# Attention scores of two heads at a time, in two PSUM banks, with new issue orders

## The chip, the cores and the metric

The kernel runs on one core of a Trainium2 chip. The time is the device time of one execution in microseconds (us), the median of three runs. TensorE is called PE here, VectorE DVE, ScalarE ACT, GpSimd POOL, and SyncE, which issues the DMAs, SP.

## What is computed

The input is x, 16 sequences of 512 rows and 128 columns, in float32. A state space block (a Mamba layer) comes first, with a normalisation before and after it, and two attention layers with feed-forward follow.

```python
x = x + _layernorm(_L0_attn_ref(_layernorm(x), ...))   # projections, convolution, a scan over 512 steps, 256 channels x 16 states
x = x + _layernorm(_L0_ffn_ref(_layernorm(x), ...))    # two layers of the kind below
# in a layer: 8 heads of 64; every block of 64 queries looks at its own 64 keys and the 64 before
sim = einsum('bhwid,bhwjd->bhwij', bq, bk)
sim = where(mask, -big, sim)
attn = softmax(sim)
out = einsum('bhwij,bhwjd->bhwid', attn, bv)
x = x + o @ wo
h = a * gelu(g)        # a, g: the halves of layernorm(shift_token(x)) @ w1 + b1
x = x + h @ w2 + b2
```

## The kernel before

The work on one sequence is cut into four streams. **E** (enter) normalises, projects and convolves, and writes the inputs of the scan to DRAM. **M** (state) is the scan: 32 steps, each an exponential on ACT (line 591), a product on POOL (643), the scan itself on DVE (615) and a second product on POOL (660), with a sum on PE (568) after every four; it ends with a normalisation into `xs`. **A** (front, the object `wf`, tiles named `f_bank`) is attention and feed-forward of layer 0, and **B** (back, `wb`, tiles named `b_bank`) the same of layer 1, and the store of the result.

In round k the kernel runs B on sequence k, A on k + 1, M on k + 2 and E on k + 3, for k from -3 to 15, so there are 14 rounds (k = 0 to 13) with A, B and M, of which the last has no E; round 14 has A and B alone, and round 15 only B. Each engine is a queue that runs strictly in the order in which the kernel issues, and `ORDER` gives that order for every engine: `A4 B1` stands for four steps of A, then one of B. `weave` carries it out. A step waits on semaphores for what it needs, and all that stands behind it on its engine waits too.

The rounds are tied to each other in four ways. A's first step, the turn of x at line 345, needs the last addition of A's feed-forward of the round before (1010) and M's normalised rows (340). B keeps its queries, keys and one bank in tiles that E uses as well: E's first PE step, the turn into `b_bank`, needs B's addition of the attention's result (line 899, `x_added`), and B of the next round needs the rows that E stored (`spilled`, the DMAs at 374 and 377). M of the next round reads these rows back before its first product.

A layer's attention has three PSUM banks (`w.banks`). For projections and rotations they are used in turn. Then they are S, PT and O. For each of eight heads PE writes the mask into S (703, bf16) and adds the scores (708): four tiles of 128 queries, each as two products with 64 rows of weights and 64 columns, that is a half of the array's rows, since a head is 64 wide, and the two halves of its columns in turn. DVE takes the row maxima (879), ACT the exponentials (818), PE turns them into PT (345), DVE or ACT copies them out (887 for even heads, 826 for odd ones), PE multiplies with the values into O (730), and DVE divides (892, 895). The scores of head i + 1 wait for the exponentials of head i, because both use S. Even heads use the first 64 partitions of keys and queries, and odd heads the last 64.

After the heads come four turns of the result (345) and their copies (830), the product with `wo` (743) and the addition (899).

Of the kernel before, what the change touches and what calls it, by code (L numbers as in the profile page):

```python
# [10 lines left out]
ALU = mybir.AluOpType  # L11
ACT = mybir.ActivationFunctionType
# [3 lines left out]
P = 128  # L16
# [30 lines left out]
    "act": (  # L47
# [4 lines left out]
    "dve": (  # L52
# [4 lines left out]
    "pool": (  # L57
        "A3 M2 A1 M1 B1 M2 A1 M2 B3 M1 B1 M2 A1 M1 B1 A1 B1 M2 B1 M1 A1 B1 A1 M2 B2 A1 B1 A1 B2 A1 B2 A1 M1 A1 M1 "
        "A1 M1 A1 M47 B1 M1 E4"),
    "sp": "M18 E1 M3 B2 S3 M1 S2",  # L60
# [40 lines left out]
def build(nc, a, out):  # L101
    with ExitStack() as ctx:
# [50 lines left out]
        class Attention:  # L153


            def __init__(self, n, banks, pr):
# [26 lines left out]
                self.scored, self.peaked, self.weighed = s("scored", 8), s("peaked", 8), s("weighed", 8)  # L183
# [492 lines left out]
        def pe_attention(E, e, b, w, l, x):  # L676
# [17 lines left out]
            S, PT, O = w.banks  # L694
            ot = O[:, 0:NT * (DH + 1)].rearrange("p (t d) -> p t d", t=NT)
            for i in range(HEADS + 2):
                if i < HEADS:
                    c, r = i // 2, DH * (i % 2)
                    if i == 0:
                        E.wait_ge(*w.qk_copied(b, 7))  # L700
                    else:
                        E.wait_ge(*w.weighed(b, i - 1))
# [542 lines left out]
```

## Time and profile before

| | |
|---|---|
| Median of three runs | 2666.77 us (2666.22 to 2666.95) |
| The profiled execution | 2667.45 us |
| Its span in the trace | 2665.7 us |
| PE, DVE, ACT, POOL busy | 2060.1, 1988.5, 1832.8, 1788.4 us |
| A full round in the middle | about 150 us |

The shares of busy time are averages over rounds with several stages. Busy time of PE is modelled at the ends of its matmuls, and a few of its records are missing. The sum below is made against 2667.45 us; the median lies 0.7 us under it.

### The profile page before, as it was taken

What the parts mean: (1) busy time and instruction counts of PE and PEld (TensorE: products, weight loads), DVE (VectorE), ACT (ScalarE), POOL (GpSimd) and SP (SyncE); (2) the same over time, 40 slices, a digit from 0 to 9 for tenths busy, and PEclk for the clock granted to TensorE, in tenths of its full rate; (3) what the DMA queues carried; (4) which work ended last, traced back from release to release, by engine and by line L of the source; (5) the groups of instructions that cost most, each with busy time, mean ns of one, the idle gap of its engine ahead of it and who ended that gap; (6) DMA issues with size and microseconds to landing.
All of it is one profiled execution on the core that took longest, in us unless ns stands there. A gap on an engine that the chain in (4) does not pass through costs nothing. (4 is left out here: it accounts for less than half of the span.)

```text
span 2665.7 us, 44136 instructions
## 1 busy us (share of the span) xinstructions
PE 2060.1 (77%) x15779; PEld 1248.1 (47%) x15936; DVE 1988.5 (75%) x3765; ACT 1832.8 (69%) x3953; POOL 1788.4 (67%) x1668
## 2 busy tenths in 40 slices
PE   2146788797978888796979888797979888786966
PEld 0013355463636455463636455463636455463734
DVE  1457696978879696978878796978878796977442
ACT  2244778787777778687777878687867878676443
POOL 0859595867859595867868595867859595863010
PEclk8567999898989999999999999999999999999877
DMA  3534323324333323324333323324333323320000
GB/s 113 142 99 107 102 74 97 97 70 120 92 112 94 96 70 100 95 69 120 92 112 92 100 68 96 94 73 119 93 112 88 100 72 93 95 72 9 5 5 8
DMA packets 107147, 231.27 MB, mean 87 GB/s; under 512 B 7728, under 2 KB 48688, under 8 KB 106672
## 3 DMA queue, kind: packets, MB, share of 16 engines
q1 hardware_dynamic: 106928, 228.44, 31.2%
q8 instruction: 126, 2.06, 0.3%
q14 instruction: 93, 0.76, 0.1%
HBM read 185.42 MB, written 42.99 MB: 86 GB/s over the span
## 5 line engine op out<-in xcount | busy, mean ns | idle before, releaser
L660 POOL TENSOR_TENSOR gy<-hs,bc 128x512 f32<-128x512 f32 x512 | 650.2, 1270 | 196.4 <-DVE hs L615 135.5
L615 DVE TENSOR_TENSOR_SCAN hs<-da,dbu 128x512 f32<-128x512 f32 x512 | 622.3, 1215 | 83.2 <-POOL dbu L643 51.4
L643 POOL TENSOR_TENSOR dbu<-spread,bc 128x512 f32<-128x512 f32 x512 | 650.3, 1272 | 22.4 <-DMA spread<-steps 22.1
L591 ACT ACTIVATE da<-spread,rest 128x512 f32<-128x512 f32 x512 | 353.3, 690 | 237.4 <-DVE hs L615 222.5
L914 POOL TENSOR_TENSOR kr<-kr,rn 128x512 f32<-128x512 f32 x256 | 264.3, 1041 | 46.4 <-ACT rn L786 35.4
L686 PE MATMUL f_bank<-rest,h_t 128*128 128x512 f32 x384 | 232.5, 707 | 70.4 <-DVE kr L859 49.2
L838 DVE TENSOR_REDUCE ss<-sq 128x8 f32<-128x512 f32 x256 | 172.4, 673 | 97.0 <-ACT sq L765 95.2
L686 PE MATMUL b_bank<-rest,h_t 128*128 128x512 f32 x384 | 227.9, 701 | 18.0 <-ACT h_t L755 12.3
L568 PE MATMUL y_sum<-gy,rest 128*32 128x512 f32 x1024 | 144.2, 637 | 96.4 <-POOL gy L660 96.4
L818 ACT ACTIVATE late<-b_bank,mx 128x128 f32<-128x128 f32 x512 | 145.9, 368 | 71.0 <-DVE mx L879 68.8
L345 PE MATMUL f_bank<-first,kr 128*128 128x128 f32 x768 | 119.8, 288 | 96.4 <-DVE kr L859 91.6
L345 PE MATMUL b_bank<-first,kr 128*128 128x128 f32 x768 | 121.4, 294 | 83.1 <-DVE kr L859 73.4
L1068 POOL TENSOR_TENSOR sq<-xs,sq 128x512 f32<-128x512 f32 x16 | 20.2, 1265 | 244.5 <-ACT xs L340 244.5
L708 PE MATMUL b_bank<-k_t,q_t 64*64 64x128 f32 x2048 | 148.6, 287 | 39.7 <-issue 15.8
L818 ACT ACTIVATE sq<-f_bank,mx 128x128 f32<-128x128 f32 x512 | 145.2, 369 | 35.3 <-DVE mx L879 35.2
L88 ACT ACT_TABLE_LOAD x112 | 143.7, 1283 | 32.9 <-DVE mv_enter L318 12.2
L345 PEld LDWEIGHTS b_bank<-first,kr 128*128 128x128 f32 x768 | 87.9, 148 | 163.4 <-DVE kr L859 124.4
L345 PEld LDWEIGHTS f_bank<-first,kr 128*128 128x128 f32 x768 | 89.3, 145 | 151.1 <-DVE kr L859 126.7
L708 PE MATMUL f_bank<-k_t,q_t 64*64 64x128 f32 x2048 | 145.8, 284 | 13.9 <-issue 5.4
L686 PEld LDWEIGHTS f_bank<-rest,h_t 128*128 128x128 f32 x384 | 75.2, 221 | 158.3 <-DVE kr L859 69.9
L686 PEld LDWEIGHTS b_bank<-rest,h_t 128*128 128x128 f32 x384 | 79.5, 225 | 119.5 <-issue 59.4
L879 DVE TENSOR_REDUCE mx<-b_bank 128x4 f32<-128x512 f32 x128 | 87.9, 687 | 59.1 <-PE b_bank L708 59.1
(176 smaller groups left out, 5009.2 us busy)
## 6 DMA issues: line engine op xcount, KB each, us to landing
spread<-steps SPq DMA_DIRECT2D x256, 512.0 KB, 4.6
steps<-k_t SPq DMA_DIRECT2D x32, 512.0 KB, 3.1
bc<-bc_rows SPq DMA_DIRECT2D x32, 512.0 KB, 7.8
gate<-gates SPq DMA_DIRECT2D x32, 512.0 KB, 5.3
gates<-kr SPq DMA_DIRECT2D x16, 512.0 KB, 3.4
gates<-late SPq DMA_DIRECT2D x16, 512.0 KB, 4.3
sq<-in_x SPq DMA_DIRECT2D x16, 256.0 KB, 3.3
x<-in_x SPq DMA_DIRECT2D x16, 256.0 KB, 4.9
```

The source lines that it names most:

```text
L88: self.e.preload_act_table_set(name)
L345: op = e.transpose(bank[:, n * P:(n + 1) * P], src(n), ident[:, :])
L568: op = e.matmul(y_sum[32 * j:32 * j + 32, :], sel[:, w, :], gy[:, 2 * j + k, :], start=w == 0 and k == 0, stop=w == 1 and k == 1, skip_gro ...
L591: e.activation(da[:, :], spread[:, slot(b, s // 2), 0, :], ACT.Exp, scale=a_neg[:, s:s + 1]).then_inc(decayed.sem, 1)
L615: e.tensor_tensor_scan(hs[:, s % 2, :], da[:, :], dbu[:, s % 2, :], 0.0, ALU.mult, ALU.add).then_inc(scanned.sem, 1)
L643: e.tensor_tensor(dbu[:, s % 2, :], spread[:, slot(b, s // 2), 1, :], bc[:, s % 2, :], ALU.mult).then_inc(fed.sem, 1)
L660: e.tensor_tensor(gy[:, s % 8, :], hs[:, s % 2, :], bc[:, 2 + s % 2, :], ALU.mult).then_inc(read_out.sem, 1)
L686: e.matmul(bank[:, :], w.h_t[:, t * P:(t + 1) * P], wqkv[:, l, part * INNER:(part + 1) * INNER], start=True, stop=True).then_inc(w.project ...
L708: op = e.matmul(S[WIN * j:WIN * j + WIN, p * P:(p + 1) * P].rearrange("p (a n) -> p a n", a=2), w.q_t[r:r + DH, c, q0:q0 + WIN], keys if j ...
L818: op = e.activation(w.pr[:, i % 2, p, :], S[:, p * P:(p + 1) * P], ACT.Exp, bias=w.mx[:, i, p:p + 1])
L838: e.tensor_reduce(w.ss[:, n, :], heads(w.sq[:, n % 2, :]), AX, ALU.add).then_inc(w.summed.sem, 1)
L914: e.tensor_tensor(x, x, w.rn[:, n, :].unsqueeze(2).to_broadcast([P, HEADS, DH]), ALU.mult).then_inc(w.normed.sem, 1)
```

## The change

The scores of heads 2g and 2g + 1 are now one step, `score(g)`. The two heads have a bank each, `X[0]` and `X[1]`, the former S and PT. PE writes the mask into both, and then issues for each tile of queries four products: two halves of columns for the even head, whose keys and queries lie in the first 64 partitions, and two for the odd head in the last 64. They use the four quarters of the array. A head's exponentials are turned into the bank in which its scores were (`turn`), and are copied out from there. `score(g)` therefore waits until the copies of both heads of the pair before are done (`p_ready`), where the scores of a head waited for the exponentials of the one before. The semaphore `scored` counts pairs. `value(hd)` holds the eight products with the values as before, `peak(hd)` and `share(hd)` the maxima and the division. Every `ORDER` string is new. The numbers of instructions on DVE, ACT and POOL for this work are the same, and PE's too.

```diff
 ORDER = {
...
-    "sp": "M18 E1 M3 B2 S3 M1 S2",
+    "sp": "M17 E1 M3 S2 M1 B1 S3 M1 B1",
...
@@ pe_attention @@
-            S, PT, O = w.banks
+            X, O = w.banks[0:2], w.banks[2]
...
+            def score(g):
+
+                if g == 0:
+                    E.wait_ge(*w.qk_copied(b, 7))
+                else:
+                    E.wait_ge(*w.p_ready(b, 2 * g - 2))
+                    E.wait_ge(*w.p_ready(b, 2 * g - 1))
+                for i in range(2):
+                    e.matmul(X[i][:, :], identb[:, :], maskb[:, :], start=True, stop=False, skip_group_check=True)
+                for p in range(NT):
+                    for j in range(2):
+                        for i in range(2):
+                            q0, r = p * P + WIN * j, DH * i
+                            keys = w.k_t[r:r + DH, g, q0:q0 + P].rearrange("p (a n) -> p a n", a=2)
+                            op = e.matmul(X[i][WIN * j:WIN * j + WIN, p * P:(p + 1) * P].rearrange("p (a n) -> p a n", a=2),
+                                          w.q_t[r:r + DH, g, q0:q0 + WIN], keys if j else keys[:, ::-1, :], start=False,
                                           stop=True, skip_group_check=True)
+                op.then_inc(w.scored.sem, 1)
+
+            def turn(hd):
+                E.wait_ge(*w.weighed(b, hd))
+                pe_turn(e, X[hd % 2], lambda n: w.pr[:, hd % 2, n, :]).then_inc(w.p_turned.sem, 1)
...
+            score(0)
+            yield
+            for g in range(HEADS // 2):
+                turn(2 * g)
+                yield
+                turn(2 * g + 1)
+                yield
+                value(2 * g)
+                yield
+                if g + 1 < HEADS // 2:
+                    score(g + 1)
                     yield
...
+                value(2 * g + 1)
+                yield
@@ act_attention @@
...
+                    op = e.activation(w.pr[:, hd % 2, p, :], X[hd % 2][:, p * P:(p + 1) * P], ACT.Exp,
+                                      bias=w.mx[:, hd, p:p + 1])
...
+                    e.activation(w.p_t[:, 1, :], X[1][:, :], ACT.Copy).then_inc(w.p_copied_act.sem, 1)
@@ dve_attention @@
...
+            for hd in range(0, HEADS, 2):
+                peak(hd)
+                yield
+                peak(hd + 1)
+                yield
+                if hd:
+                    yield from share(hd - 1)
...
+                e.tensor_copy(w.p_t[:, 0, :], X[0][:, :]).then_inc(w.p_copied.sem, 1)
+                yield
+                yield from share(hd)
+            yield from share(HEADS - 1)
```

Three places show how the new orders move instructions. The first is PE early in the heads of stream B. `b_bank<-maskb` and `b_bank<-k_t,q_t` are mask and scores, `b_bank<-first,late` is the turn of a head's exponentials, `b_bank<-vs,m` and `<-v,m` the product with the values, `f_bank` is the same for stream A. Before, from B's second head on:

```order
L703 MATMUL b_bank<-maskb,identb 128x512
L708 MATMUL b_bank<-k_t,q_t 64x128 x8
L345 MATMUL f_bank<-first,kr 128x128 x4
L345 MATMUL b_bank<-first,late 128x128 x4
L345 MATMUL f_bank<-first,kr 128x128 x4
L703 MATMUL b_bank<-maskb,identb 128x512
L708 MATMUL b_bank<-k_t,q_t 64x128 x8
L703 MATMUL f_bank<-maskb,identb 128x512
L708 MATMUL f_bank<-k_t,q_t 64x128 x8
L345 MATMUL b_bank<-first,late 128x128 x4
```

And of after, from B's second pair on:

```order
L706 MATMUL b_bank<-maskb,identb 128x512 x2
L712 MATMUL b_bank<-k_t,q_t 64x128 x16
...
L345 MATMUL f_bank<-first,kr 128x128 x4
L345 MATMUL b_bank<-first,late 128x128 x4
L345 MATMUL f_bank<-first,kr 128x128 x4
L345 MATMUL b_bank<-first,late 128x128 x4
L345 MATMUL f_bank<-first,kr 128x128 x4
```

Stream A's scores now begin after B's third pair, where they began behind B's third head.

The second place is PE at the end of stream A's heads. `b_bank<-first,q_t` is the turn with which stream E begins, `L433` its first projection, `f_bank<-first,sq` the turn of the exponentials of A's last head, `f_bank<-first,kr` the turns of A's result and `L743`, later `L757`, the product with `wo`. Before:

```order
L568 MATMUL y_sum<-gy,rest 32x512 x4
L345 MATMUL f_bank<-first,sq 128x128 x4
L345 MATMUL b_bank<-first,q_t 128x128 x4
L730 MATMUL f_bank<-vs,m 64x65
L730 MATMUL f_bank<-v,m 64x65
...
L433 MATMUL b_bank<-m,first 128x512
L730 MATMUL f_bank<-vs,m 64x65
```

And of after, where the first row belongs to the value product of A's last head:

```order
L730 MATMUL f_bank<-vs,m 64x65
...
L345 MATMUL f_bank<-first,kr 128x128 x8
L345 MATMUL b_bank<-first,q_t 128x128 x4
L345 MATMUL f_bank<-first,kr 128x128 x8
L433 MATMUL b_bank<-m,first 128x512
L757 MATMUL f_bank<-rest,q_t 128x128 x16
L345 MATMUL b_bank<-first,sq 128x128 x4
L958 MATMUL f_bank<-xs,rest 128x256
```

The turn of E moved from between A's last turn and its last two value products to behind the whole of A's last head and two turns of the result.

The third place is ACT at the end of a round. `L483`, `L488` and `L491` belong to E's step sizes, the rows on `kr` (990, later 1011) are A's gelu, `mv_y` and `mv_x` M's statistics, `mv_out` those of B's result. Before:

```order
L88 ACT_TABLE_LOAD
L990 ACTIVATE kr<-f_bank,rest 114x512 x2
L483 ACTIVATE m<-b_bank,first 128x512
L990 ACTIVATE kr<-f_bank,rest 113x512
L88 ACT_TABLE_LOAD
L488 ACTIVATE m<-m 128x512 x2
L491 ACTIVATE m<-m 128x512 x2
L325 ACTIVATE lv_x<-mv_x,columns 128x4
L329 ACTIVATE rs_x<-lv_x 128x4
L340 ACTIVATE xs<-x,mr_x,rs_x 128x128 x4
```

And of after:

```order
L491 ACTIVATE m<-m 128x512 x2
L88 ACT_TABLE_LOAD
L1011 ACTIVATE kr<-f_bank,rest 114x512
L1011 ACTIVATE kr<-f_bank,rest 113x512
L88 ACT_TABLE_LOAD
L325 ACTIVATE lv_x<-mv_x,columns 128x4
L325 ACTIVATE lv_out<-mv_out,columns 128x4
L329 ACTIVATE rs_out<-lv_out 128x4
L329 ACTIVATE rs_x<-lv_x 128x4
L340 ACTIVATE xs<-xs,mr_out,rs_out 128x128 x4
L340 ACTIVATE xs<-x,mr_x,rs_x 128x128 x4
```

E's exponentials and logarithms moved ahead of A's last two gelus, B's last normalisation moved to directly before M's, and a full round has six table loads in place of seven.

## Rows read from the trace of the kernel before

**Rows 1.** The page, part 1: busy us (share of the span), instructions.

```profile
PE 2060.1 (77%) x15779; PEld 1248.1 (47%) x15936; DVE 1988.5 (75%) x3765; ACT 1832.8 (69%) x3953; POOL 1788.4 (67%) x1668
```

**Rows 2.** Timeline, start of two rounds: start, us, engine, line, [idle<-releaser].

```profile
1060.19 0.63 PE L345 MATMUL f_bank<-first,xs 128*128 128x128 f32 x4 [0.87 <-DVE xs L1010]
1065.64 0.63 PE L345 MATMUL b_bank<-first,xs 128*128 128x128 f32 x4 [0.70 <-DMA steps<-k_t]
...
1208.72 1.65 ACT L340 ACTIVATE xs<-x,mr_x,rs_x 128x128 f32<-128x128 f32 x4 [0.29 <-DVE mr_x L334]
1209.70 0.69 DVE L1010 TENSOR_TENSOR xs<-xs,f_bank 128x512 f32<-128x512 f32 x1 [1.08 <-PE f_bank L961]
1210.54 0.63 PE L345 MATMUL f_bank<-first,xs 128*128 128x128 f32 x4 [0.87 <-DVE xs L1010]
1212.25 0.36 SPq L377 DMA_DIRECT2D steps<-k_t  x1
```

**Rows 3.** Busy by stretch: us, PE, PEld, DVE, ACT, POOL (x instructions), PEclk, DMA.

```profile
1060.20:1114.90 54.70, 37.97 (x140) 17.95 (x145) 48.81 (x72) 35.65 (x73) 44.01 (x50) 0.91 0.42 113
1114.90:1172.00 57.10, 51.22 (x673) 37.93 (x683) 49.60 (x96) 44.59 (x116) 51.69 (x43) 1.00 0.40 105
1172.00:1210.50 38.50, 35.19 (x178) 20.14 (x178) 24.45 (x66) 34.10 (x60) 16.11 (x14) 1.00 0.15 50
```

**Rows 4.** Timeline: first maxima, E's turn, A's last value product and wo.

```profile
1114.93 0.69 DVE L879 TENSOR_REDUCE mx<-b_bank 128x4 f32<-128x512 f32 x1 [0.22 <-PE b_bank L708]
...
1167.35 0.66 PE L345 MATMUL b_bank<-first,q_t 128*128 128x128 f32 x4
...
1171.77 0.22 PE L730 MATMUL f_bank<-v,m 128*64 128x65 f32 x1
```

**Rows 5.** Timeline: one head of stream B.

```profile
1116.85 0.39 PE L703 MATMUL b_bank<-maskb,identb 128*128 128x512 bf16 x1 [0.97 <-ACT late L818]
1117.17 1.09 PE L708 MATMUL b_bank<-k_t,q_t 64*64 64x128 f32 x16
1118.31 0.69 DVE L879 TENSOR_REDUCE mx<-b_bank 128x4 f32<-128x512 f32 x1 [0.23 <-PE b_bank L708]
1119.04 1.14 ACT L818 ACTIVATE late<-b_bank,mx 128x128 f32<-128x128 f32 x4 [0.16 <-DVE mx L879]
```

**Rows 6.** Groups by line and shape: busy us, mean ns, idle before.

```profile
L708 PE MATMUL b_bank<-k_t,q_t 64*64 64x128 f32 x2048 | 148.6, 287 | 39.7 <-issue 15.8 <-ACT late L818 12.1 <-ACT k_t L794 9.8
L615 DVE TENSOR_TENSOR_SCAN hs<-da,dbu 128x512 f32<-128x512 f32 x512 | 622.3, 1215 | 83.2 <-POOL dbu L643 51.4 <-issue 15.9 <-ACT da L591 14.5
L313 DVE BATCH_NORM_STATS2 stat_ff<-sq 128x6 f32<-128x128 f32 x128 | 27.8, 279 | 40.9 <-ACT sq L973 40.9
L88 ACT ACT_TABLE_LOAD x112 | 143.7, 1283 | 32.9 <-DVE mv_enter L318 12.2 <-DVE mv_out L318 6.2 <-PE b_bank L952 3.3
```

**Rows 7.** Waits of DVE from 1114.9 to 1172: us in total, times, longest.

```profile
DVE mx L879 <- PE b_bank L708: 1.9, 5, 0.7
DVE mx L879 <- PE f_bank L708: 1.2, 3, 0.7
```

**Rows 8.** Round 14, timeline of DVE: first maxima of B, last division of A.

```profile
2458.95 0.69 DVE L879 TENSOR_REDUCE mx<-b_bank 128x4 f32<-128x512 f32 x1 [2.01 <-PE b_bank L708]
...
2517.65 0.18 DVE L892 RECIPROCAL rd<-f_bank 128x4 f32<-128x4 f32 x1 [0.87 <-PE f_bank L730]
```

**Rows 9.** Busy by stretch in rounds 14 and 15, as rows 3.

```profile
2460.00:2480.00 20.00, 18.19 (x144) 14.04 (x148) 6.99 (x13) 7.98 (x27) 1.04 (x1) 0.57 0.01 1
...
2590.60:2628.00 37.40, 32.26 (x278) 24.63 (x279) 12.53 (x26) 11.18 (x36) 0.00 (x0) 0.52 0.00 1
```

**Rows 10.** Round 15, timeline of DVE: the maxima, then the last division.

```profile
2590.68 0.69 DVE L879 TENSOR_REDUCE mx<-b_bank 128x4 f32<-128x512 f32 x1 [5.60 <-PE b_bank L708]
2595.16 0.69 DVE L879 TENSOR_REDUCE mx<-b_bank 128x4 f32<-128x512 f32 x1 [3.79 <-PE b_bank L708]
...
2628.13 0.18 DVE L892 RECIPROCAL rd<-b_bank 128x4 f32<-128x4 f32 x1 [0.87 <-PE b_bank L730]
```

More of the change, by code:

```diff
@@ new lines, in turn, with value @@
+            def turn(hd):
+                E.wait_ge(*w.weighed(b, hd))
+                pe_turn(e, X[hd % 2], lambda n: w.pr[:, hd % 2, n, :]).then_inc(w.p_turned.sem, 1)
+            def value(hd):
+                E.wait_ge(*w.p_ready(b, hd))
+                E.wait_ge(*w.v_paired(b, NT - 1))
+                E.wait_ge(*w.v_before(b, NT - 2))
+                if hd:
+                    E.wait_ge(*w.o_done(b, hd - 1))
+                for p in range(NT):
+                    for j in range(2):
+                        q0 = p * P + WIN * j
+                        op = e.matmul(ot[WIN * j:WIN * j + WIN, p, :], w.p_t[:, hd % 2, q0:q0 + WIN],
+                                      (w.vs, w.v)[j][:, p, hd, :], start=True, stop=True)
+                op.then_inc(w.valued.sem, 1)
@@ L808, in act_attention @@
                     yield
-            S, PT, O = w.banks
-            for i in range(HEADS + 1):
-                if i < HEADS:
-                    E.wait_ge(*w.peaked(b, i))
-                    if i > 1:
-                        E.wait_ge(*w.p_turned(b, i - 2))
-                    E.use_table(EXP_LN)
-                    for p in range(NT):
-                        op = e.activation(w.pr[:, i % 2, p, :], S[:, p * P:(p + 1) * P], ACT.Exp, bias=w.mx[:, i, p:p + 1])
-                    op.then_inc(w.weighed.sem, 1)
-                    yield
-                hd = i - 1
-                if hd > 0 and hd % 2:
+            X = w.banks[0:2]
+            for hd in range(HEADS):
+                E.wait_ge(*w.peaked(b, hd))
+                if hd > 1:
+                    E.wait_ge(*w.p_turned(b, hd - 2))
+                E.use_table(EXP_LN)
+                for p in range(NT):
+                    op = e.activation(w.pr[:, hd % 2, p, :], X[hd % 2][:, p * P:(p + 1) * P], ACT.Exp,
+                                      bias=w.mx[:, hd, p:p + 1])
+                op.then_inc(w.weighed.sem, 1)
+                yield
+                if hd % 2:
                     E.wait_ge(*w.p_turned(b, hd))
@@ L829, in act_attention @@
                 E.wait_ge(*w.o_turned(b, c))
-                e.activation(w.o_t[:, c, :], (S, PT)[c % 2][:, :], ACT.Copy).then_inc(w.o_copied.sem, 1)
+                e.activation(w.o_t[:, c, :], X[c % 2][:, :], ACT.Copy).then_inc(w.o_copied.sem, 1)
                 yield
@@ new lines, in peak, with share @@
+            def peak(hd):
+                E.wait_ge(*w.scored(b, hd // 2))
+                e.tensor_reduce(w.mx[:, hd, :], X[hd % 2][:, :].rearrange("p (t k) -> p t k", t=NT), AX, ALU.max,
+                                negate=True).then_inc(w.peaked.sem, 1)
+            def share(hd):
+                E.wait_ge(*w.valued(b, hd))
+                e.reciprocal(w.rd[:, hd, :], ot[:, :, DH]).then_inc(w.inverted.sem, 1)
+                yield
+                E.wait_ge(*w.inverted(b, hd))
+                e.tensor_tensor(w.o[:, :, hd * DH:(hd + 1) * DH], ot[:, :, 0:DH],
+                                w.rd[:, hd, :].unsqueeze(2).to_broadcast([P, NT, DH]), ALU.mult).then_inc(w.o_done.sem, 1)
+                yield
@@ new lines, in dve_attention @@
+            for hd in range(0, HEADS, 2):
+                peak(hd)
+                yield
+                peak(hd + 1)
+                yield
+                if hd:
+                    yield from share(hd - 1)
+                E.wait_ge(*w.p_turned(b, hd))
+                if hd:
+                    E.wait_ge(*w.valued(b, hd - 2))
+                e.tensor_copy(w.p_t[:, 0, :], X[0][:, :]).then_inc(w.p_copied.sem, 1)
+                yield
+                yield from share(hd)
+            yield from share(HEADS - 1)
```

69 lines of the change are left out of this document (5 added, 64 removed), and 22 rows, old and new, of the table ORDER.

## The prediction, written before the run

> **What bounds the kernel now.** The busy shares come first: PE 77%, DVE 75%, ACT 69%, POOL 67% [rows 1]. No engine is full, so the question is what ties the rounds together. The timeline where two rounds meet answers it. A full round is 1210.54 - 1060.19 = 150.3 us. At its end three chains arrive almost at once: M's normalised rows (1208.72 + 1.65 = 1210.37), the end of A (1209.70 + 0.69 = 1210.39), and E's last store, issued at 1212.25, for whose like B's first turn waited at 1065.64 [rows 2]. Shortening one chain alone gives nothing.
>
> I cut the round at two places, B's first row maxima (1114.93) and A's last product with the values (ends at 1172.0) [rows 4], and read the busy time of each stretch [rows 3]. Stretch 1 (54.7 us) is projections and rotations: DVE is busy 48.8 us, PE only 38.0. Stretch 2 (57.1 us) holds all heads: PE 51.2, POOL 51.7, DVE 49.6. Stretch 3 (38.5 us) is the feed-forward of both layers, nearly all of E and the end of M: PE 35.2, ACT 34.1, DVE 24.5. The change shortens PE's work in stretch 2, where it is one of three nearly full engines, and moves work among all three.
>
> **PE's work.** One head's scores are 16 records of mean 287 ns that together take 1.09 us [rows 5, 6]: the two column halves already run side by side. In no row do two halves of the array's rows run side by side. If the second head of a pair is hidden whole, a pair costs 1.09; if not at all, 2.18. I take 1.09, since the column halves hide each other whole, and keep 2.18 as a rival. The Trainium skill's page TensorEngine Tiling (Array Packing), section Theoretical Speedup, gives up to a factor of two for each dimension of 64 or less; by the columns alone, which is all that the trace shows, nothing would be saved, and by the page the second factor comes too. With 1.09, eight pairs a round save 8 x 1.09 = 8.7 us of PE. The masks cost the same as before, 0.32 each [rows 5].
>
> **The waits of a pair.** Before, two heads in a row take 2 x (0.32 + 1.09 + 0.69 + 1.14) = 6.5 us of mask, scores, maxima and exponentials [rows 5], 6.7 with the hops. Now it is two masks, one set of scores, the first maxima, two heads' exponentials, the odd head's turn (0.66, rows 4) and its copy, which I price like the maxima, a pass over the same 512 columns: 0.64 + 1.09 + 0.69 + 2.28 + 0.66 + 0.69 = 6.1, 6.3 with hops. The new wait on `p_ready` thus costs no time against the old one, 0.4 us less a pair. Behind the waiting scores on PE stand the values of the odd head and A's steps; DVE waits for them.
>
> **Stretch 1.** Two of A's rotation steps on DVE, 0.66 each, come after B's first maxima instead of ahead of them. DVE's 48.8 becomes 47.5. Around it lie the start-up (A's first projection and square, some 3.7 us in which DVE has nothing) and some 1.5 us for B's last keys. That gives 52.7, so -2.0. Bounds: 0 and -2.5.
>
> **Stretch 2.** DVE gains the two rotation steps (+1.3) and loses one scan (-1.2, rows 6) and B's feed-forward statistics (four of 0.28 and the small steps behind them, -1.6, rows 6), so 49.6 - 1.5 = 48.1 us. Its idle time was 57.1 - 49.6 = 7.5 us, of which 3.1 waited for scores [rows 7]. With PE at 51.2 - 8.7 = 42.5 us, PE no longer presses and most of that 3.1 goes; the rest stays, because A's last two pairs now run without B beside them and each is a chain of 6.3 us and more. I take 4.8 us idle: 52.9, so -4.2. Bounds: 3 us idle (-6.0) and 7.5 (-1.5).
>
> **Stretch 3.** Before, E's turn started at 1167.35, 4.6 us ahead of the cut [rows 4], and from there to the next round's start it is 43.2 us [rows 2, 4]. Now the turn stands behind A's last values and two turns of its result. DVE must first do a scan (1.2) and the last division, then PE two turns: 2.7 us behind the cut. The chain from there loses one table load of 1.28 (seven a round, 112 in 16 [rows 6], become six). The result is 2.7 + 43.2 - 1.3 = 44.6, so +6.1. For: E's exponentials stand ahead of A's last gelus. Against: B's last normalisation stands directly ahead of M's on ACT, and A's now follows SiLU of E. I keep 42 and 47 as bounds. The new place of B's result on POOL, last in the round, costs nothing: POOL is busy 16.1 of 38.5 us there [rows 3].
>
> A round: -2.0 - 4.2 + 6.1 = -0.1 us. PE's 8.7 us are gained in stretch 2 only as far as DVE allows and are given back by E's late start. Fourteen rounds: -1 us.
>
> **The last two rounds** have no M and no E, so DVE's limit and E's late start are both absent. In round 15 B runs alone at half clock (0.52, that is mostly 1.2 of 2.4 GHz [rows 9]). Maxima follow each other in 4.5 us (2590.68, 2595.16), and to the last division it is 37.4 us [rows 10]. A pair was 9.0 and is now 1.2 (masks) + 1.97 (scores at half clock, an estimate from 1.09) + 0.69 + 2.28 + 1.1 + 0.69 = 7.9, 8.1 with hops. Three pairs and the end of the fourth (some 6) give 30.3: -7. In round 14 the same stretch is 58.7 us [rows 8], 20 us of it at clock 0.57 with PE busy 18.2 [rows 9]. Now A's scores start after two of B's pairs and the third's scores (some 16 us), three pairs of A follow at some 8.5, and the fourth takes some 7: 49, so -10. Bounds -4 and -15. Together -17.
>
> **Forecast**: 2667.45 - 1 - 17 = 2649; against the median 0.7 less, 2648 us.
>
> **The rivals.**
>
> *The cut comes through.* DVE's idle time in stretch 2 falls to 3 us and stretch 3 is 43: a round is -2 - 6 + 4.5 = -3.5, and the time 2667 - 49 - 17 = 2601. For it speaks that PE is busy 35.2 of 38.5 us in stretch 3, so that whatever it sheds ahead helps. Against it, DVE.
>
> *E starts late and nothing is made up* (the slower side). E's chain goes through every engine in order. If the table load saved does not lie on it, and A's normalisation and last gelus wait behind E's SiLU and B's gelu, stretch 3 is 47: a round is +2.3, the sum +32 - 17 = +15, 2682 us. It is slower than before from 45.9 us of stretch 3 on. The three arrivals within 2 us [rows 2] speak for it.
>
> *The row halves do not overlap.* A pair costs 1.09 more, DVE keeps 7.5 us idle, a round is +2.6, and in the last round a pair is 10.1 against 9.0. That gives 2667 + 36 + 4 = 2707.
>
> *The clock falls in the heads.* It fell to 0.57 and 0.52 where M and E were absent [rows 9], and stretch 2 now has less of PE's work. If half of a round's heads run at 1.2 GHz as in round 14, some 8 us of PE come back: +3.5 a round, 2667 + 49 - 10 = 2706. Against it, stretch 1 with PE busy 38.0 of 54.7 keeps 0.91 [rows 3].
>
> **How the numbers follow.** Chances: forecast (2627 to 2662) 0.40, cut comes through 0.19, E late 0.23, no overlap 0.08, clock 0.10. The range reaches from 2603 to 2697: it leaves out nearly half of the first rival and most of the last two, 0.2 in all. About 0.2%, 5 us, is what can be told from no change. Faster by more than that: 0.38 of the forecast's 0.40 and the first rival's 0.19, so 0.57. Within it: the forecast's rest and the near end of E late, 0.11. Slower: 0.32. Cases of both signs share the chance; the likeliest one's own range is 2627 to 2662.
>
> **What would show it.** Right: 32 score records of a pair within some 1.1 us; PE's busy time 120 to 150 us less; stretches near 52.7, 52.9 and 44.6; E's turn behind A's last values; 96 table loads; round 15 shorter by 7 us. Wrong: a score step of 2 us; clock under 0.95 in stretch 2; a stretch 3 under 42 us or over 47.

## The result, and the profile after

The kernel after takes 2584.3 us (2582.7 to 2585.6, 4 runs) against 2666.5 (2664.9 to 2667.0, 4 runs) for the kernel before beside it: a ratio of 0.969, 95% interval 0.968 to 0.971. The forecast was 2648 with a range from 2603 to 2697. The gain is 82 us where 19 were forecast, and the time lies 19 us below the range.

Page of the kernel after, part 1 (busy us, share of the span, instructions) and the granted clock in 40 slices; they answer to [rows 1]:

```profile
PE 1929.1 (75%) x15808; PEld 1115.1 (43%) x15936; DVE 1973.0 (76%) x3765; ACT 1786.7 (69%) x3937; POOL 1785.1 (69%) x1668
PEclk9986899999999999998999999999999999999977
```

PE is busy 131 us less (120 to 150 were forecast). Beyond that DVE is down 15.5 us and ACT 46, of which 20.5 are sixteen table loads.

The round that answers to [rows 3], cut at the same places (round start, B's first maxima, end of A's last value product, next start). Columns: us, PE, PEld, DVE, ACT, POOL with instructions, granted clock, DMA share, GB/s:

```profile
1039.40:1091.00 51.60, 33.50 (x141) 15.01 (x143) 47.01 (x72) 32.68 (x67) 41.19 (x46) 0.97 0.43 107
1091.00:1141.70 50.70, 44.68 (x665) 31.46 (x671) 46.46 (x87) 39.42 (x107) 48.12 (x43) 1.00 0.38 100
1141.70:1184.80 43.10, 37.15 (x185) 21.27 (x186) 28.32 (x78) 39.06 (x73) 22.31 (x18) 1.00 0.25 81
```

A round is 145.4 us: 51.6 + 50.7 + 43.1. Against 54.7 + 57.1 + 38.5 that is -3.1, -6.4 and +4.6. The forecast had -2.0, -4.2 and +6.1. All three signs are right, and all three sizes err to the same side. Over the thirteen full rounds (0 to 12) the means are 54.4, 56.8 and 38.7 before and 51.7, 50.8 and 43.0 after: -2.7, -6.0 and +4.3. The round shown in [rows 3] has a longer second stretch than most (57.1 where 56.7 is usual).

The pair of heads, the timeline of PE and DVE (start, us, engine, line), against [rows 5]:

```profile
1096.77 0.38 PE L706 MATMUL b_bank<-maskb,identb 128*128 128x512 bf16 x1 [0.16 <-issue]
1097.08 1.10 PE L712 MATMUL b_bank<-k_t,q_t 64*64 64x128 f32 x32
...
1098.25 1.29 DVE L892 TENSOR_REDUCE mx<-b_bank 128x4 f32<-128x512 f32 x2
```

The 32 records of a pair take 1.10 us, as the 16 of one head took 1.09: the halves of the rows hide each other whole.

Where two rounds meet, the timeline of PE, SyncE's queue and POOL, against [rows 2, 4]:

```profile
1143.86 0.60 PE L345 MATMUL b_bank<-first,q_t 128*128 128x128 f32 x4
...
1180.71 0.36 SPq L377 DMA_DIRECT2D steps<-k_t  x1
...
1184.75 0.63 PE L345 MATMUL f_bank<-first,xs 128*128 128x128 f32 x4 [0.87 <-DVE xs L1031]
1185.21 0.60 PE L345 MATMUL b_bank<-first,xs 128*128 128x128 f32 x4
...
1193.57 1.27 POOL L643 TENSOR_TENSOR dbu<-spread,bc 128x512 f32<-128x512 f32 x1 [9.56 <-DMA spread<-steps]
```

E's turn does stand 2.2 us behind the cut, but E's last store is issued 36.9 us after it (1180.71 - 1143.86), where it took 44.9 before (1212.25 - 1167.35 [rows 2, 4]). So it comes 4.0 us ahead of the next round's start; before, it came 1.7 behind it. B's first turn follows A's at once (1185.21), where it waited for that store's data until 5.4 us after the start [rows 2]. A's start itself waits for A's own sum for 0.87 us in both kernels, so the store sets when B starts, and not when A does.

The two last rounds, where heads run without M and E (stretches from B's first maxima to the last division; round 14, then 15), against [rows 8 to 10]:

```profile
2390.13 1.29 DVE L892 TENSOR_REDUCE mx<-b_bank 128x4 f32<-128x512 f32 x2 [0.57 <-PE b_bank L712]
...
2436.28 0.18 DVE L898 RECIPROCAL rd<-f_bank 128x4 f32<-128x4 f32 x1 [0.93 <-PE f_bank L730]
```

And of the stretches:

```profile
2390.00:2436.00 46.00, 39.47 (x627) 30.55 (x632) 26.31 (x59) 28.21 (x87) 2.95 (x4) 1.00 0.01 2
2513.70:2542.30 28.60, 19.65 (x259) 14.41 (x262) 11.89 (x26) 11.09 (x36) 0.00 (x0) 0.74 0.00 1
```

They are 46.2 and 28.6 us where 58.7 and 37.4 were: -12.5 and -8.8, forecast -10 and -7. Between the two stretches 4.4 us are given back: from A's last division in round 14 to B's maxima in round 15 (2513.72) it is 77.4 us for 73.0, at a granted clock of 0.79 for 0.87.

The whole difference follows from the round starts. These are A's first turns in rounds 0 and 13 of the kernel before, then of after:

```profile
312.36 0.66 PE L345 MATMUL f_bank<-first,xs 128*128 128x128 f32 x4 [1.21 <-ACT xs L340]
2261.59 0.63 PE L345 MATMUL f_bank<-first,xs 128*128 128x128 f32 x4 [0.87 <-DVE xs L1010]
```

```profile
313.00 0.63 PE L345 MATMUL f_bank<-first,xs 128*128 128x128 f32 x4 [0.87 <-DVE xs L1031]
2204.56 0.63 PE L345 MATMUL f_bank<-first,xs 128*128 128x128 f32 x4 [0.87 <-DVE xs L1031]
```

Thirteen full rounds took 1949.2 us and take 1891.6: -57.6, -4.4 each. The spans end at 2665.7 and 2580.2, so what follows them took 404.1 us and takes 375.6: -28.5. What precedes them is the same within 1 us. (The spans differ by 85.5 us, the medians by 82.)

What follows is rounds 13 to 15, and round 13 is a case of its own: it has A, B and M, but no E. It took 148.6 us and takes 139.3, so -9.3, and the last two rounds together -19.1. The forecast counted round 13 among fourteen rounds of -0.1 us. So it missed 56 us in the full rounds, 9 in round 13 and 2 in the last two. The third stretch of round 13, before and then after, in the columns of [rows 3]:

```profile
2373.10:2410.20 37.10, 30.35 (x164) 19.86 (x164) 18.95 (x58) 25.34 (x44) 13.20 (x11) 0.94 0.07 22
```

```profile
2306.60:2343.80 37.20, 29.22 (x166) 18.13 (x165) 21.90 (x69) 26.64 (x52) 16.83 (x14) 1.00 0.12 30
```

Without E this stretch does not grow, though DVE has 3 us more to do in it and ACT 1.3. With E it grows by 4.3 us. (The granted clock is 0.94 in one and 1.00 in the other, so a part of a microsecond may be hidden in this.)

### The profile page after: what moved, and what is told of

Read it like the earlier page. It is cut to its first block, busy times and chain, and to the rows that moved or that the text cites. A ratio compares the mean times of both kernels' runs of the same rounds, so it can differ in the third digit from the quotient of the medians.

```text
span 2580.2 us, 44117 instructions
## 1 busy us (share of the span) xinstructions
PE 1929.1 (75%) x15808; PEld 1115.1 (43%) x15936; DVE 1973.0 (76%) x3765; ACT 1786.7 (69%) x3937; POOL 1785.1 (69%) x1668
## 4 chain that ended last, share of the span: by engine, by line
POOL 25%; DVE 25%; ACT 18%; PE 16%; issue 9%; DMA 5%; SPq 1%; POOLq 0%; DVEq 0%; ACTq 0%
POOL gy L660 9%; POOL dbu L643 8%; DVE hs L615 7%; POOL kr L935 5%; ACT late L831 3%; ACT da L591 3%; DMA x<-in_x 3%; DVE mx L892 3%; PE b_bank L345 2%; DVE ss L851 2%; PE b_bank L712 2%; DVE m L860 2%; PE f_bank L345 2%; ACT sq L831 2%; ACT L88 1%
## 5 line engine op out<-in xcount | busy, mean ns | idle before, releaser
L686 PE MATMUL b_bank<-rest,h_t 128*128 128x512 f32 x384 | 238.9, 733 | 93.9 <-DVE kr L872 76.1
L686 PE MATMUL f_bank<-rest,h_t 128*128 128x512 f32 x384 | 213.9, 662 | 25.9 <-ACT h_t L769 14.0
L671 POOL TENSOR_TENSOR x<-gy,x 128x512 f32<-128x512 f32 x16 | 20.4, 1276 | 191.0 <-DVE gy L628 191.0
L345 PE MATMUL f_bank<-first,sq 128*128 128x128 f32 x576 | 93.4, 285 | 24.0 <-ACT sq L831 23.9
L345 PE MATMUL b_bank<-first,late 128*128 128x128 f32 x512 | 81.1, 287 | 34.9 <-ACT late L831 34.9
```

What stands on the lines that cost most here:

```text
L345: op = e.transpose(bank[:, n * P:(n + 1) * P], src(n), ident[:, :])
L686: e.matmul(bank[:, :], w.h_t[:, t * P:(t + 1) * P], wqkv[:, l, part * INNER:(part + 1) * INNER], start=True, stop=True).then_inc(w.project ...
```

## The experiments

The kernel before took 2657 to 2663 us in the four groups of runs, and a second run of the kernel after agrees with the first.

> The kernel after itself, unchanged, on the chip of this job, as the base for the three others. If chips differ little, 2584 us as at first, a ratio of 0.969 to 0.971; if the kernel after is touchier than the one before (the kernel before takes 2657 to 2667 on three chips), up to 2600.

Measured 2582.0 us, ratio 0.971 (0.968 to 0.973). I compare with 2583 us below. Most rounds of the kernel after repeat to 0.2 us (51.6, 50.7, 43.1), so that stretches tell more than times. In some variants rounds of two lengths take turns; where that matters it is said.

**1. The heads in turn, not side by side.**

```diff
-                for p in range(NT):
-                    for j in range(2):
-                        for i in range(2):
+                for i in range(2):
+                    for p in range(NT):
+                        for j in range(2):
```

> The changed kernel, with all orders and banks as they are, but the eight score products of the even head stand on PE ahead of the eight of the odd head, so that the two heads' row halves no longer take turns. If PE's time in the heads is what the change is worth (theory Q, the quarters), a score step takes about 2.0 us in place of 1.10, PE's busy time grows by some 8 x 16 x 1.0 = 130 us, a round grows by 3 to 5 us and the time lies at 2635 to 2665. If the new orders carry the gain (theory O), the time stays within 2584 to 2610. If the halves overlap in this order too, the score step stays near 1.1 us and the time at 2584.

Measured 2639.4 us, ratio 0.992 (0.990 to 0.995). The timeline of PE and the stretches of a round of this kernel:

```profile
968.89 1.59 PE L712 MATMUL b_bank<-k_t,q_t 64*64 64x128 f32 x32
```

And of the stretches:

```profile
910.70:962.70 52.00, 33.83 (x140) 15.36 (x141) 46.99 (x71) 32.79 (x67) 41.52 (x46) 0.97 0.43 106
962.70:1016.30 53.60, 47.81 (x667) 34.99 (x672) 46.87 (x87) 39.38 (x107) 47.74 (x42) 1.00 0.36 95
1016.30:1059.40 43.10, 37.14 (x186) 21.24 (x185) 28.36 (x78) 39.10 (x73) 22.34 (x18) 1.00 0.25 81
```

The same sixteen products take 1.59 us when a head's sixteen records come in a row, 1.10 when the heads alternate. That is 0.49 us x 128 pairs = 63 us of PE, and the time rose by 56: PE's score step has a price of 0.9 us a microsecond. For the 3.9 us of PE added in a round, stretch 2 grows by 2.9 us and stretch 1 by 0.4.

**2. The scores twice.** The sixteen products of a pair are issued once more ahead of the masks.

```diff
+                for p in range(NT):
+                    for j in range(2):
+                        for i in range(2):
+                            ...
+                            e.matmul(X[i][...], w.q_t[...], keys ..., start=True, stop=True, skip_group_check=True)
                 for i in range(2):
                     e.matmul(X[i][:, :], identb[:, :], maskb[:, :], start=True, stop=False, skip_group_check=True)
```

> The kernel after, in which the sixteen score products of a pair are issued a second time ahead of the masks (their result is overwritten by the mask, so the output is the same). A pair costs PE 1.10 us more, 128 pairs in all: 141 us of PE. It is as if the halves of the rows did not overlap. Theory 1: the end of the program follows PE's score step nearly one to one in the heads; with the heads in turn a pair took 1.59 us in place of 1.10 and the time rose 55 us for 63 us of PE, 0.88 a microsecond. Then this kernel takes 2584 + 0.88 x 141 = 2708 us (2690 to 2725). Theory 2: DVE is what limits the heads and PE only touches it: the first half microsecond cost what it did by chance of the order, and the rest is partly hidden: under 2660.

Measured 2710.9 us, ratio 1.020 (1.018 to 1.022). Theory 1 holds: +128 us for 141 of PE, 0.91. Stretch 2 of this kernel:

```profile
1757.10:1814.60 57.50, 52.72 (x896) 37.52 (x896) 47.01 (x87) 39.51 (x107) 47.19 (x42) 1.00 0.34 89
```

+6.8 for 8.8 us of scores, DVE's busy time up by 0.5. PE costs this kernel what the row halves would cost if they did not overlap. So without that overlap the change would be 2% slower than the kernel before, and the rival's 2707 us was near the right price for it.

**3. More work for DVE.**

```diff
                 E.wait_ge(*w.inverted(b, hd))
+                e.tensor_reduce(w.spare[:, hd % 2, :], ot[:, :, 0:DH], AX, ALU.max)
                 e.tensor_tensor(w.o[:, :, hd * DH:(hd + 1) * DH], ot[:, :, 0:DH],
```

> The kernel after, with one more reduction on DVE for each head, ahead of the division, over the 256 elements of the head's values, into a spare tile of its own: 16 a round at about 0.41 us (the division reads as many elements and takes 0.41), 6.6 us of DVE a round, 105 us in all. Theory 1 (the prediction's: DVE is the limit of the second stretch, it idles only 4.2 of 50.7 us there): nearly all of it comes through, 2665 to 2690. Theory 2: the way through the heads is the chain mask, scores, maxima, exponentials, and DVE's work besides it fits in: under 2620.

Measured 2638.0 us, ratio 0.993 (0.991 to 0.995), between the two theories. The added reduction takes 0.42 us, 107 us in all, and 55 of them come through. A round is 149.4 us, its stretch 2:

```profile
964.20:1019.40 55.20, 47.18 (x672) 32.28 (x672) 51.58 (x102) 39.75 (x108) 48.58 (x43) 0.97 0.35 94
```

Here stretch 2 grew by 4.5 us for the 6.7 added (DVE's busy time rose by 5.1, the rest overlaps). But the granted clock is 0.97 in it, and PE is busy 47.2 us for 44.7 with the same work. In some rounds the clock stays at 1.00, and there it is 54.0 us:

```profile
1563.60:1617.60 54.00, 45.97 (x672) 31.44 (x671) 51.48 (x102) 39.80 (x108) 48.49 (x43) 1.00 0.36 97
```

That is +3.3 us for 6.7, the same 0.5 a microsecond as over the whole program, and some 1.2 us of the 4.5 come with the lower clock. DVE has a price too, then, but it is no lid over PE: its idle time is 3.6 us in the first of these rounds and 2.5 in the second, under the 4.8 that the forecast left it.

**4 and 5. Orders and heads apart.** The first kernel has the heads of after and the `ORDER` strings of before (on PE the first pair's scores stand at the place of its first head's and most later ones at that of the second head's, where the expectation has the first for all; each turn stands where it can). The second has the heads of before and the strings of after.

> The changed code of the heads, both banks and the quarters, with the orders of the kernel before: the strings of DVE, ACT, POOL and SP word for word, PE's with the score steps of a pair merged at the place of the first one. Theory Q: PE is relieved as in the changed kernel, and the time is near it, 2584 to 2620. Theory O: it is near the kernel before or above it, 2650 to 2700, because the old orders put A's and B's heads where the new banks make them wait for the copies of a pair.

> The heads of the kernel before, one at a time in one bank, with the orders of the changed kernel: DVE, ACT, POOL and SP word for word, PE's with each pair's score step split into two around the turn. Theory Q: no gain or a loss, 2660 to 2720. Theory O: most of the gain is there, 2590 to 2630.

Measured 2958.1 us, ratio 1.113 (1.110 to 1.116), and 3135.9 us, ratio 1.182 (1.176 to 1.188). Both miss both theories. The stretches of the first:

```profile
1000.60:1054.50 53.90, 37.19 (x157) 17.10 (x162) 48.76 (x73) 36.06 (x74) 44.23 (x50) 0.94 0.43 116
1054.50:1133.70 79.20, 54.76 (x658) 38.36 (x657) 50.65 (x96) 43.23 (x115) 51.81 (x44) 0.81 0.29 75
1133.70:1172.60 38.90, 35.40 (x181) 20.26 (x180) 24.61 (x66) 34.43 (x60) 15.81 (x13) 1.00 0.15 50
```

And of the second:

```profile
871.80:923.10 51.30, 34.40 (x123) 15.70 (x125) 46.97 (x71) 32.62 (x67) 40.87 (x45) 0.93 0.43 108
923.10:1012.30 89.20, 69.67 (x680) 51.54 (x689) 48.06 (x87) 40.24 (x107) 48.52 (x43) 0.75 0.22 57
1012.30:1055.40 43.10, 37.15 (x185) 21.28 (x186) 28.32 (x78) 39.04 (x73) 22.29 (x18) 1.00 0.25 81
```

They cannot price the orders of the heads, since queues in an order made for other steps wait for each other there (and the granted clock falls to 0.81 and 0.75 while PE waits). But they part the terms: stretches 1 and 3 are those of the kernel whose strings they have (53.9 and 38.9 with the old, 51.3 and 43.1 with the new), whatever the heads do. So -3.1 and +4.6 belong to the orders, and only stretch 2 to both.

**6. E's turn early.** On PE the step with E's turn is moved from behind two turns of A's result to ahead of A's last but one value product, about where it was before.

> The changed kernel with one step moved: E's first turn on PE stands ahead of the last two value products of A, where it was before the change. My sum priced its new place at about +6 us a round in the last stretch (stretch 3 was 38.5 us before, is 43.1 now). If the late turn costs that, this kernel gains 2 us or more a round, 2530 to 2560. If the turn is late because ACT and DVE have E's other steps late as well, nothing changes: 2578 to 2590.

Measured 2648.5 us, ratio 0.996 (0.994 to 0.997): 65 us slower than after. The turn in this kernel:

```profile
1025.15 1.12 PE L332 MATMUL b_bank<-first,q_t 128*128 128x128 f32 x4 [3.73 <-ACT q_t L327]
```

And its second stretch:

```profile
973.10:1029.50 56.40, 46.82 (x669) 33.08 (x676) 48.09 (x87) 40.64 (x110) 49.43 (x44) 0.97 0.38 99
```

PE stands 3.7 us in front of the turn, since ACT normalises E's input later in the new order. Behind it stand A's value products. The round starts at 920.69, so the turn comes 104.5 us behind the start, just as in the kernel after (1143.86 - 1039.41): it stands earlier in the queue and comes no earlier. Stretch 2 becomes 56.4 us, stretch 3 41.7, so 5.7 are lost ahead of the cut for 1.4 behind it. About 2 of the 5.7 us come with the clock, since PE is busy 46.8 us for 44.7 at a granted clock of 0.97. So moving PE's step alone gains nothing; what an earlier start of E as a whole would be worth, this kernel does not show.

**7. The old tail.** Behind A's last head PE, ACT and DVE follow in the order of the kernel before.

> The kernel after, but behind A's last head the steps of PE, ACT and DVE follow in the order of the kernel before (on PE E's turn stands directly behind A's last value product, ahead of the turns of A's result; on ACT seven table loads a round in place of six), and POOL adds B's result ahead of M's. Theory 1: in the kernel after E's last store is issued 4 us ahead of the next round's start, so E's chain binds nothing and its earlier turn gives nothing; the new order of the tail is worth the table load and one or two us more for A's feed-forward and M's normalisation: 2584 + 16 x (1.3 to 3) = 2605 to 2632. Theory 2 (the prediction's): E's late turn costs, and the earlier turn gives about 1 us a round less the table load: 2575 to 2595.

Measured 2725.7 us, ratio 1.026 (1.024 to 1.028), worse than either theory. A round of this kernel and the store in question:

```profile
317.60:373.80 56.20, 37.81 (x141) 16.73 (x142) 46.95 (x70) 32.65 (x67) 43.04 (x47) 0.88 0.43 117
373.80:427.10 53.30, 45.75 (x672) 31.52 (x672) 46.77 (x87) 41.04 (x111) 49.24 (x43) 1.00 0.39 105
427.10:472.60 45.50, 38.68 (x186) 22.18 (x185) 27.46 (x78) 38.64 (x70) 19.59 (x16) 0.93 0.12 37
```

And of its timeline:

```profile
474.32 0.36 SPq L364 DMA_DIRECT2D steps<-k_t  x1
```

E's turn comes at 427.50, 1.8 us sooner after the cut, and still the last store is issued 46.8 us behind it (36.9 in the kernel after), 1.7 us behind the next start at 472.60. B's channels come to ACT 8.0 us behind the start (480.62). Stretch 3 is 2.4 us longer, with one more table load of 1.28 in it and a granted clock of 0.93, stretch 2 is 2.6 us longer and stretch 1 4.6. In all this kernel takes 9.6 us more a round. In the kernel with all the old strings (experiment 4) the same tail has a third stretch of 38.9 us, so this, too, is a queue in an order made for other steps, and no price of E's place.

**8. The loads of M ahead of the last store.** In the kernel after M's first product waits for loads that stand behind the store of B's result on the DMA queue.

```diff
-    "sp": "M17 E1 M3 S2 M1 B1 S3 M1 B1",
+    "sp": "M2 O1 M15 E1 M3 S2 M1 B1 S3 M1",
```

(`O` is the store of B's result of the round before.)

> The kernel after, with the store of B's result behind the first loads of M's next round on the DMA queue, where those loads stood behind it (they were issued at 1039.20 and 1039.83, the store at 1038.72, and M's first product on POOL waited 7.6 us for them). The loads need E's last store, which lands about 2.8 us after 1035.39. Theory 1: they are issued up to 1.6 us earlier and the start of the scans follows by as much, or partly: 2560 to 2580. Theory 2: the first stretch is set by A's and B's projections and rotations on DVE, and the DMA engines are full there anyway (9 tenths and more in most slices): no change, 2580 to 2588.

Measured 2608.9 us, ratio 0.982 (0.980 to 0.984): slower by 26, which neither theory had. Both halves of the reason are in the timeline; the round starts at 1046.41:

```profile
1045.82 0.58 SPq L1100 DMA_DIRECT2D out_dram<-sq  x1
...
1051.50 1.27 POOL L643 TENSOR_TENSOR dbu<-spread,bc 128x512 f32<-128x512 f32 x1 [5.84 <-DMA spread<-steps]
...
1052.10 0.59 ACT L767 ACTIVATE h_t<-b_bank 64x512 f32<-64x512 f32 x1 [1.20 <-DMA out_dram<-sq]
```

M's product is 5.1 us behind the start, 1.8 sooner than in the kernel after at 1039.41 (1046.30), as planned. But the store now lands behind two loads of 512 KB, and ACT, which wants its buffer for B, waits for it until 5.7 us. The same two places in the kernel after, start at 1039.41:

```profile
1038.72 0.38 SPq L1098 DMA_DIRECT2D out_dram<-sq  x1
...
1042.98 0.58 ACT L767 ACTIVATE h_t<-b_bank 64x512 f32<-64x512 f32 x1
```

**9 to 11. The last microseconds, and one load ahead.** First, on DVE A's last two gate steps ahead of the statistics of B's result, and on ACT M's rows ahead of B's:

```diff
-    "dve": "... E1 M1 A1 B1 M1 B2 A2 B1 M1 A1"
+    "dve": "... E1 M1 A1 B1 M1 A2 B2 M1 B1 A1"
-    "act": "... E2 A2 M1 B2 M1 B1 M1"
+    "act": "... E2 A2 M2 B2 M1 B1"
```

(Only the ends of the two strings are shown.)

> The kernel after with another order in the last 6 us of a round: on DVE A's last two gate steps (0.7 each) ahead of the statistics of B's result, on ACT M's normalised rows ahead of B's. Theory 1: the next round starts when A's feed-forward and M's rows are both there (in the kernel after at 1039.27 and 1038.89), and E's chain, whose last store is issued at 1035.39, has no part in it. A's end comes 1.2 us earlier, M's too: 1.2 us a round, 2584 - 17 = 2567 (2562 to 2574). Theory 2: B's result, now 2.2 us later, binds the next round, since the same buffer is wanted by B's first squares and the first loads of M stand behind its store on the DMA queue: 2584 to 2610.

Measured 2604.8 us, ratio 0.979 (0.977 to 0.982). The time fits theory 2: stretch 3 gains less than 1 us, but B's result is late, and with it its store and the loads behind that store. The round starts at 900.83:

```profile
903.16 0.38 SPq L1085 DMA_DIRECT2D out_dram<-sq  x1
...
905.69 0.59 ACT L754 ACTIVATE h_t<-b_bank 64x512 f32<-64x512 f32 x1 [0.42 <-DMA out_dram<-sq]
...
910.97 1.27 POOL L630 TENSOR_TENSOR dbu<-spread,bc 128x512 f32<-128x512 f32 x1 [7.83 <-DMA spread<-steps]
```

M's first product is 10.1 us behind the start, B's channels 4.9 (3.6 in the kernel after), and stretch 1 is 53.6. Second, only the load that depends on nothing late ahead of the store (`"sp": "M1 O1 M16 ..."`); third, both:

> As the kernel with the loads first, but only one load (B's rows of E, which wait for nothing of the last stores) stands ahead of the store of B's result; the loads of the spread steps stand behind it as in the kernel after. With both loads ahead, M's first product came 1.8 us earlier, but the store took over 5 us behind a megabyte of loads, and ACT waited for it until 5.7 us after the round's start. Theory 1 (the store's landing is what cost 24 us): it lands in time here, and the earlier load is worth 0 to 1 us a round: 2568 to 2584. Theory 2 (any load ahead delays the store by about as much as it moves): 2590 to 2610.

Measured 2582.0 us, ratio 0.971 (0.968 to 0.974), the same as after. The harm of experiment 8 was the store's landing. M's first product came 5.1 to 6.7 us behind the starts here, 6.7 to 8.8 in the kernel after, and that gained nothing: so early, M's start is covered.

> The two edits together. If B's late result binds the next round by way of the loads behind its store, the load ahead of it takes part of that back: faster than the new end alone by up to 1 us a round. If both gains come through: 2584 - 17 - 8 = 2559 us. If the store lands too late for B's first squares: slower than the new end alone, 2580 to 2600.

Measured 2592.6 us, ratio 0.975 (0.972 to 0.978): 12 us of the new end's 22 come back. B starts as late as with the new end alone, and M's first product comes at 7.8 us in place of 10.0, so at this point M's start does count. No variant beats the kernel after.

**12. E's last store late.** By itself:

```diff
-    "sp": "M17 E1 M3 S2 M1 B1 S3 M1 B1",
+    "sp": "M17 E1 M3 S2 M1 B1 S2 M1 B1 S1",
```

> The kernel after, in which only E's last store (du) stands behind M's and B's stores on the DMA queue: it is issued at about 0.3 us ahead of the next round's start in place of 4.0 ahead, some 3.7 us later, and lands where that of the kernel before did. Nothing else is moved. Theory 1: the first stretch was 54.7 us in the kernel before and is 51.6 after mainly because the store comes earlier, so that B's first turn need not wait for it and M's first product stands 6.9 us behind the round's start in place of 10.8. Then stretch 1 grows by 2 to 3.5 us and the time by 30 to 52 us: 2613 to 2635. Theory 2 (the prediction's): the stretch is shorter because two of A's rotation steps on DVE come behind B's first maxima; the store's time is hidden: under 2595.

Measured 2623.4 us, ratio 0.985 (0.983 to 0.987), +40 us, in the range of theory 1. A round of this kernel:

```profile
606.30:661.40 55.10, 37.15 (x140) 16.64 (x142) 47.00 (x71) 32.44 (x67) 41.18 (x45) 0.88 0.43 110
661.40:712.10 50.70, 44.70 (x665) 31.50 (x672) 46.45 (x87) 39.37 (x107) 48.12 (x43) 1.00 0.38 100
712.10:755.20 43.10, 37.13 (x186) 21.25 (x185) 28.36 (x78) 39.09 (x73) 22.35 (x18) 1.00 0.22 69
```

And of its timeline:

```profile
610.10 1.08 PE L332 MATMUL b_bank<-first,xs 128*128 128x128 f32 x4 [3.13 <-DMA steps<-k_t]
610.98 2.95 PE L673 MATMUL f_bank<-rest,h_t 128*128 128x512 f32 x4
...
613.56 0.69 DVE L838 TENSOR_REDUCE ss<-sq 128x8 f32<-128x512 f32 x1 [7.20 <-ACT sq L766]
```

Only stretch 1 moved, by 3.5 us, to about what it was in the kernel before. But it got there another way. The new order of PE starts with `A1 B1`, the old one with `A4 B1`. So in the new order a late store holds B's turn, and A's first projection stands right behind it on PE: it starts 4.6 us behind the round's start (610.98 - 606.34), and DVE's first reduction 7.2. In the kernels before and after the same reduction comes at 3.7, first before, then after:

```profile
1063.89 0.69 DVE L838 TENSOR_REDUCE ss<-sq 128x8 f32<-128x512 f32 x1 [3.69 <-ACT sq L765]
```

```profile
1043.12 0.69 DVE L851 TENSOR_REDUCE ss<-sq 128x8 f32<-128x512 f32 x1 [3.70 <-ACT sq L779]
```

The late store of the kernel before held B alone, since three of A's projections stood ahead of B's turn. So this experiment shows what a late store costs the new order. It does not show what the earlier store gave against the old one.

Stretch 1 can be read as three terms: the time until DVE's first reduction, DVE's busy time, and the rest of its idle time. These are medians over rounds 1 to 12 of each kernel, in us, the first three columns behind the round's start:

| kernel | DVE's first reduction | first copy of B's turn on ACT | M's first product | DVE busy | rest of its idle time | stretch 1 |
|---|---|---|---|---|---|---|
| after | 3.7 | 3.6 | 7.2 | 47.0 | 0.9 | 51.6 |
| one load first | 3.7 | 3.6 | 5.4 | 46.9 | 0.9 | 51.6 |
| both | 3.9 | 4.7 | 7.8 | 47.1 | 1.0 | 52.4 |
| loads first | 3.7 | 5.8 | 5.2 | 47.1 | 2.1 | 53.1 |
| new end | 3.9 | 4.7 | 10.0 | 47.2 | 2.6 | 53.6 |
| before | 3.7 | 6.0 | 10.7 | 48.8 | 2.2 | 54.8 |
| store late | 7.1 | 7.0 | 8.4 | 46.9 | 0.9 | 55.0 |
| old tail | 8.1 | 8.0 | 11.5 | 47.0 | 0.9 | 56.0 |

With the store late and with the old tail nearly the whole loss against the kernel after is the first term. With the loads first and with the new end it is the rest: in the one B starts late, in the other M's first product above all, and "both" against "new end", with B's start the same, gives 1.2 us for M's alone. From before to after the first term stands still, DVE's busy time falls by 1.8 and the rest by 1.3.

## Why the prediction was wrong, point by point

**PE's work.** Right. A pair in 1.10 us, 8.7 us a round, the row halves hidden whole. The Trainium skill's page TensorEngine Tiling (Array Packing), section Theoretical Speedup, gives up to a factor of two for a dimension of 64 or less. For the rows the trace agrees (1.10 us for a pair against 2 x 1.09), on condition that the products of the four quarters alternate: with the heads in turn it was 1.59 us, a factor of 1.4 over one head after the other.

**Stretch 2, the failed step: -4.2 forecast, -6.4 measured (-6.0 in the mean).** The prediction made DVE the limit: 48.1 us of its work and 4.8 idle, so that of PE's 8.7 us only a part of the 3.1 in which DVE waited for scores could come through. Both parts were off. DVE's busy time fell by 3.1 us (49.6 to 46.5), where 1.5 was counted. Summed over its instructions the work fell by 2.1: one scan -1.2, B's feed-forward statistics -1.7 and the small step behind them -0.4, two steps of a rotation +1.4, and all others -0.1. The other 1.0 is that its records overlap more. And DVE is not the limit: PE's scores cost 0.9 us for each microsecond added, by 0.49 and by 1.10 a pair, and DVE's work 0.5 (experiments 1 to 3). So no engine bounds the stretch alone, and most of what is taken from PE is gained. By experiment 2 the overlap is worth 7.8 us a round, of which 6.8 in stretch 2. That this stretch gained only 6.0 to 6.4 leaves a loss of 0.4 to 0.8 for the rest of the change there (pairs that wait for both copies, the new order, E's and B's steps moved out), which was not taken apart further.

**Stretch 1, mis-sized: -2.0 forecast, -3.1 measured (-2.7 in the mean).** The sum was 3.7 us of start-up, 47.5 of DVE and 1.5 of other idle time, 52.7. The three terms measured 3.7, 47.0 and 0.9, 51.6. So the mechanism held: DVE sheds two of A's rotation steps (1.3 of the 1.8 us by which it is less busy; the other 0.5 was not taken apart), and the start-up stays. In the kernel before the third term was 2.2. Why it fell by 1.3 is open. B starts 2.4 us sooner and M's first product comes 3.5 us sooner than before, and in the kernels with the loads first and with the new end lateness of either costs about as much. But experiment 12 does not test it, since the late store there holds A as well.

**Stretch 3, the other large miss: +6.1 forecast, +4.6 measured (+4.3 in the mean).** The prediction took "E's turn to next start, 43.2 us" as one chain that shifts with the turn, less one table load of 1.3. The turn comes 2.2 us behind the cut, 2.7 forecast, and from it to the next start it is 40.9 us (1184.75 - 1143.86), 41.9 forecast: that is 0.5 and 1.0 too much. And the chain is not rigid: from the turn to E's last store it is 36.9 us and was 44.9, and the store is issued 4.0 us ahead of the start, where it was 1.7 behind. That the stretch grows is the new orders' doing: it is 38.9 with the old strings and 43.1 with the new whatever the heads do (experiments 4 and 5). And it takes E: in round 13, which has none, the stretch is as long as before. Whether E costs there by its late start or by its work in it (ACT is busy 39.1 of 43.1 us) is open, since in experiment 6 the turn came no earlier, and in experiment 7 the old tail did not fit the rest of the order.

**Round 13** has no E, so nothing of the +6.1 applies to it. The forecast gave it -0.1 like the others, and it is -9.3.

**The last two rounds.** The mechanism was right, the sizes small: -12.5 and -8.8 against -10 and -7. In round 14 the granted clock, 0.57 for 20 us before, stayed at 1.00. In round 15 the forecast took a pair at half clock, 8.1 us; the three pairs take 8.1, 7.4 and 7.4, at a granted clock of 0.74 where it was 0.52. That the clock would rise was not forecast, so a part of the 8.8 us is luck.

**The table loads** are 96, as forecast. **The clock** in stretch 2 is 1.00, so that rival had no part in it. **The other rivals.** "The cut comes through" was nearest (2601): it had 3 us idle in stretch 2 and 43 for stretch 3. The idle time is 4.2, stretch 3 is 43.1, and stretch 1 gave 1 us more. It was given 0.19, with DVE's load as what spoke against it.

**Summed:** each full round was forecast at -0.1 us and is -4.4 in the mean, -57.6 for thirteen. Of the 4.3 us missed a round, 1.8 lie in stretch 2, 0.7 in stretch 1 and 1.8 in stretch 3. Round 13 adds 9 and the last two rounds 2.

## What to carry to other kernels

When several engines are each busy for 80 to 95% of a stretch, do not make one of them the lid: ask for the price of each, by adding a known amount of work to it. Here the prices stood side by side, 0.9 for PE and 0.5 for DVE, and a change of the granted clock had to be kept out of the second. A chain's length is no constant of the kernel: if the order of its steps among others is new, follow it to its last store again, and then ask what the next stage waits for. Before a delay in the new kernel is read as what the old one suffered, look at what stands behind the waiting step in each order: here it was A's first projection in the one and nothing of A's start in the other. And where several transfers meet, the order of their issue sets when each lands, the harmless one included.

## What the runs showed of the hardware

Sixteen products of 64 rows by 64 columns on four quarters take 1.10 us when the quarters alternate and 1.59 us when one head's quarters (two columns of one row half) come first and the other's follow. The expectation for the second was 2.0 us: the halves of the rows still overlap in part when they do not alternate. A store of 256 KB that lands within 4.3 us of its issue in the kernel after (1038.72, no wait at 1042.98) took 6.3 us behind two loads of 512 KB (1045.82, waited for until 1052.10). And the granted clock fell to 0.81 and 0.75 in a stretch in which PE was busy 54.8 of 79.2 and 69.7 of 89.2 us but waited often, while with 44.7 of 50.7 it was 1.00.
